# A graph layer and a routed feed-forward in one kernel: the first eight quads of pass one from an early table

## The reference, cut to what matters

```
# layer 1: graph aggregation, then a recurrence over the 128 steps
beta = (layernorm(x) @ e_weight) / max(sum(adj, axis=2), 1e-7)
agg  = einsum('blu,blm->bmu', beta, adj)
h    = tanh(agg[:, t] @ Wx + h @ Wh + b)          # for t = 0 .. 127
x    = x + all the h
# layer 2: 16 experts, the best two per token
y      = layernorm(x)
logits = y @ gate_w + gate_b;  w, idx = softmax/top_k(logits, 2)
moe    = sum over the two of  w * (relu(y @ w1[e] + b1[e]) @ w2[e] + b2[e])
x      = x + layernorm(y + moe) * gamma + beta
```

## Time and profile before

| | |
|---|---|
| median of 3 runs | 655.46 us |
| the profiled execution's own time | 655.11 us |
| its span, first to last instruction | 653.4 us |
| busy: PE, DVE, ACT, POOL | 535.4, 507.6, 411.0, 451.3 us |
| stage B, scatters of POOL | 99 to 264 us |
| pass one, scatters of POOL | 276 to 454 us |
| pass two, scatters of POOL | 471.5 to 648.5 us |

### The profile page before, as it was taken

One profiled execution on the slowest core, in us unless ns is written; L12 is line 12 of the kernel. 1 busy time (PEld: TensorE's weight loads), 2 busy tenths in 40 slices (PEclk: granted clock), 3 DMA queues, 4 the chain that ended last, 5 costly groups with the idle time before them and its releaser, 6 DMA issues. The chain is left out here.

```text
span 653.4 us, 17215 instructions
## 1 busy us (share of the span) xinstructions
PE 535.4 (82%) x4144; PEld 476.4 (73%) x4144; DVE 507.6 (78%) x2512; ACT 411.0 (63%) x1343; POOL 451.3 (69%) x521
## 2 busy tenths in 40 slices
PE   1676799999889861799999999943899999999990
PEld 0566567776666650599999999941799999988890
DVE  4899269999999997488888888620499899898861
ACT  1898765555555533366666666710589889899860
POOL 8766307777777777277777777776177777777775
PEclk9988899889999965899999999975799999999995
DMA  8999913665355214479886665442997666764110
GB/s 208 254 285 271 287 50 102 213 200 170 118 168 114 88 54 124 111 241 346 264 257 198 208 199 188 153 157 72 338 332 246 216 200 204 220 187 140 48 54 15
DMA packets 112893, 119.26 MB, mean 183 GB/s; under 512 B 18346, under 2 KB 97406, under 8 KB 112801
## 3 DMA queue, kind: packets, MB, share of 16 engines
q1 hardware_dynamic: 93056, 73.55, 40.6%
q0 software_dynamic: 17152, 43.03, 18.1%
q10 hardware_dynamic: 2592, 1.64, 0.8%
HBM read 66.51 MB, written 53.77 MB: 184 GB/s over the span
## 5 line engine op out<-in xcount | busy, mean ns | idle before, releaser
L311 POOL DMA_INDIRECT out_dram<-R x136 | 135.0, 993 | 59.4 <-issue 52.2
L311 POOL DMA_INDIRECT rows_by_second<-R x136 | 136.2, 1001 | 54.2 <-issue 33.2
L311 POOL DMA_INDIRECT rows_by_first<-st x128 | 125.9, 984 | 64.4 <-issue 35.6
L1143 PE MATMUL bank<-xT,wr 128*128 128x128 f32 (+1 forms) x1152 | 155.6, 280 | 8.9 <-ACT xT L1218 8.9
L1163 PE MATMUL bank<-W,hs 128*128 x1024 | 156.9, 290 | 0.0
L1143 PEld LDWEIGHTS bank<-xT,wr 128*128 128x128 f32 x1152 | 140.8, 194 | 16.0 <-ACT xT L1218 16.0
L1243 ACT ACTIVATE hs<-bank,wr 128x128 f32<-128x128 f32 x380 | 111.8, 366 | 64.4 <-PE bank L1143 59.3
L1163 PEld LDWEIGHTS bank<-W,hs 128*128 128x128 f32 x1024 | 135.1, 192 | 3.1
L1228 ACT COPY wr<-W1b 128x258 f32 x288 | 103.5, 424 | 0.0
L1328 DVE SCALAR_TENSOR_TENSOR R<-bank,R 128x128 f32<-128x128 f32 x272 | 82.2, 344 | 24.5 <-PE bank L1163 24.5
L670 ACT ACTIVATE HT<-bank,bcol 128x128 f32<-128x128 f32 x128 | 47.0, 367 | 66.6 <-PE bank L573 65.6
(11 more groups left out here) (171 smaller groups left out, 896.2 us busy)
## 6 DMA issues: line engine op xcount, KB each, us to landing
R<-rows_by_second SPq DMA_DIRECT2D x122, 196.0 KB
R<-rows_by_first SPq DMA_DIRECT2D x124, 68.0 KB
xq<-in_x_dram SPq DMA_DIRECT2D x32, 256.0 KB, 4.1
aq<-in_adj_dram SPq DMA_DIRECT2D x32, 256.0 KB, 5.0
x2r<-in_x_dram SPq DMA_DIRECT2D x32, 256.0 KB, 2.9
rows_by_second<-filler SPq DMA_DIRECT2D x2, 1568.0 KB, 7.4
rows_by_second<-filler SPq DMA_DIRECT2D x16, 196.0 KB
rows_by_second<-R POOLq DMA_INDIRECT x136
```

Of the source, the lines that this page charges most:

```text
L311: return nc.gpsimd.indirect_dma_start(dst, bass.IndirectOffsetOnAxis(ap=idx, axis=0), src, None, bounds_check=limit[n], oob_is_err=False)
L1143: i = mm(ps_h[c][h][:, at:at + n], wr[:, u % 2, s, j, c * P:(c + 1) * P], xT[:, u % 2, j * P + lo:j * P + lo + n], start=True, stop=True)
```

## The change

Pass one begins before stage B has ended everywhere. After quad 24 of 32 has been placed (`SEEN = 24`), DVE works out an early table of the blocks that are already full (`early_a`, `early_b`), for 32 blocks (`TAKEN`), which are the first eight quads of pass one (`EARLY = 8`). SP loads them as soon as the scatters of the first 24 quads have landed. The full tables are worked out later, by DVE inside pass one: `table_a` after its quad 3, `table_b` after its quad 5. Quads from 8 on use them. With it:

- The bias splitting (`biases`) moves into stage B, behind step 9. A new small instruction per pair of quads (`shift`) prepares -mean/std.
- In pass one `zed` moves from DVE to ACT, and ACT's relus of pass one move to DVE.
- All 16 filler blocks of the first list are now issued by SP; ACT issued half.
- ACT clears the buffers for mixed quads inside pass one, at its quad 12.
- No idle multiplications ahead of pass one; three instead of one behind the wait ahead of pass two.
- In pass two, the first quad is normalised at once, and not during the second quad.

The core of the diff:

```diff
+    SEEN, EARLY = 24, 8
+    TAKEN = EARLY * QUAD
@@ sp_stages
+            sp.wait_ge(early_tables, 1)
+            for u in range(SLOTS):
+                sp.wait_ge(s_sct[u], 64 * SEEN // SLOTS)
+            for q in range(EARLY):
+                for j, row in enumerate(numbers(sp, sti[0:1, 0, QUAD * q:QUAD * q + QUAD], ROWS - P)):
+                    load(sp, 0, q, j, row)
             sp.wait_ge(starts, 1)
             pad(sp, 0)
+            pad(sp, 8)
@@ dve_stages
+            def shift(p):
+                dve.wait_ge(s_r2, p + 1)
+                v.scalar_tensor_tensor(out=two(p, C_SHIFT), in0=two(p, C_MEAN), scalar=-1.0, in1=two(p, C_RSTD),
+                                       op0=ALU.mult, op1=ALU.mult)
             for t in range(0, NQ + 4, 2):
                 even(t)
                 odd(t + 1)
+                if t == 8:
+                    biases()
+                if t + 1 == SEEN + 3:
+                    early_a()
+                if t + 1 == SEEN + 5:
+                    early_b()
@@ sp_passes
-                rows = [numbers(sp, sti[0:1, r, QUAD * q:QUAD * q + QUAD], ROWS - P) for q in range(AHEAD)]
-                begin(sp, r, rows, (0, 1))
-                for q in range(AHEAD, NQUAD):
+                if r:
+                    rows = [numbers(sp, sti[0:1, r, QUAD * q:QUAD * q + QUAD], ROWS - P) for q in range(AHEAD)]
+                    begin(sp, rows, (0, 1))
+                else:
+                    landed(sp, 0)
+                for q in range(AHEAD if r else EARLY, NQUAD):
                     quad(r, q, q + NQUAD * r, (q + NQUAD * r) % RING)
                     if r == 0 and q == RING - 1:
                         pad_b(sp)
@@ pe_passes
-            pe.wait_ge(tables, 1)
+            pe.wait_ge(early_tables, 1)
+            pe.wait_ge(s_pos, NQ)
...
+                landed(pe, 1)
+                warm(3)
...
+                if G == EARLY:
+                    pe.wait_ge(tables, 1)
...
+                if G == 4:
+                    codes()
@@ act_passes
+            def zed(G, u):
+                act.wait_ge(e_ld[u], loads_of(G))
+                for j in range(QUAD):
+                    i = a(R[:, u, j, C_Z:W_B], R[:, u, j, 0:P], ACT.Identity,
+                          scale=R[:, u, j, C_RSTD:C_RSTD + 1], bias=R[:, u, j, C_SHIFT:C_SHIFT + 1])
+                i.then_inc(e_z, 1)
+            def quad_0(q, G, u, last):
...
+                if q == EARLY - 1:
+                    act.wait_ge(tables, 1)
+                if q == RING:
+                    zeros_for_mixed()
+                e = experts(0, q + 1)
+                v = (u + 1) % RING
+                zed(G + 1, v)
+                weights(0, q + 1, G + 1, v, 0, e)
+                weights(0, q + 1, G + 1, v, 1, e)
+                turn_out(G + 1, v)
+                weights(0, q + 1, G + 1, v, 2, e)
+                weights(0, q + 1, G + 1, v, 3, e)
@@ dve_passes
+            def quad_0(q, G, u, last):
...
+                relu(G, u, 0)
+                if q > 1:
+                    share(0, G - 1, before, 1)
+                relu(G, u, 1)
+                if q > 0:
+                    add_beta(G, u)
+                share(0, G, u, 0)
...
+                if q == 3:
+                    table_a()
+                if q == 5:
+                    table_b()
+            def quad_1(q, G, u, last):
...
+                if q == 0:
+                    norm_b(G, u, 0)
+                    share(1, G, u, 1)
+                    norm_a(G, u, 1)
+                    norm_b(G, u, 1)
```

More of the change, by code:

```diff
@@ L1040, in passes @@
+            return table_a, table_b
         def passes(eng, body):
@@ L1184, in quad @@
                     second(r, G, 0, e[2:4])
+                    second(r, G, 1, experts(r, at + QUAD)[0:2])
                 if not last:
@@ L1257, in experts, with begin_pass @@
                 return e + numbers(act, et_act[0:1, r, at + QUAD:at + 2 * QUAD]) if mixed(q) else e
-            def quad(r, q, G, u, last):
-                start = isinstance(q, int) and q == 0
-                if start:
-                    e = experts(r, q)
-                    for j in range(QUAD):
-                        weights(r, q, G, u, j, e)
-                    loads(r)
-                    turn_out(G, u)
-                if r == 0 and q == NPURE:
+            def begin_pass(r, q, G, u):
+                e = experts(r, q)
+                for j in range(QUAD):
+                    weights(r, q, G, u, j, e)
+                if r:
+                    loads()
+                else:
+                    zed(G, u)
+                turn_out(G, u)
@@ L1268, in quad @@
+            def quad_1(q, G, u, last):
+                start = q == 0
+                if start:
+                    begin_pass(1, q, G, u)
+                if q == NPURE:
                     act.wait_ge(e_mix, 2)
-                e = None if last else experts(r, q + 1)
+                e = None if last else experts(1, q + 1)
                 v = (u + 1) % RING
-                relu(r, G, u, 0)
-                if r == 1 and not start:
+                relu(G, u, 0)
+                if start:
+                    relu(G, u, 1)
+                elif q > 1:
@@ L1273, in quad @@
                     root(G - 1, 0)
+                if not last:
+                    weights(1, q + 1, G + 1, v, 0, e)
+                    weights(1, q + 1, G + 1, v, 1, e)
                 if start:
-                    relu(r, G, u, 1)
-                if not last:
-                    weights(r, q + 1, G + 1, v, 0, e)
-                    weights(r, q + 1, G + 1, v, 1, e)
-                if not start:
-                    relu(r, G, u, 1)
+                    root(G, 0)
+                else:
+                    relu(G, u, 1)
@@ L1281, in quad @@
                 if not last:
                     turn_out(G + 1, v)
-                    weights(r, q + 1, G + 1, v, 2, e)
-                    weights(r, q + 1, G + 1, v, 3, e)
-                if r == 1 and not start:
+                    weights(1, q + 1, G + 1, v, 2, e)
+                    weights(1, q + 1, G + 1, v, 3, e)
+                if q > 1:
                     root(G - 1, 1)
-                if last and r == 1:
+                if start:
+                    root(G, 1)
+                if last:
```

387 lines of the change are left out of this document (227 added, 160 removed).

## The result

The changed kernel takes 667.87 us (median of 4 runs, 666.71 to 668.58) where the kernel before takes 655.61 on the same chip (654.96 to 658.24): ratio 1.0187, 95% interval 1.0163 to 1.0212. It is 1.9% slower. The forecast of 659.5 had the direction; the time lies above the range of 648.5 to 666.

The account below looks back on a forecast made before the run. POOL, issuing scatters, was taken to bound the kernel. On 655.11 us: start +0.3, stage B +6.5, first gap -12.0, pass one +13.1, start of pass two -3.6 gave 659.4, as median 659.5; range 648.5 to 666.

Parts of the forecast that it names:

- (g): Pass one, SP: loads wait for `table_b`, quad 12's also for `pad_b`; POOL stalls 3 us at quad 11.
- (h): Pass one, ACT: clearing buffers for 7.1 us at quad 12 costs 4.8 us, of which 4 are counted.
- (e): Pass one, DVE: `table_a` takes 7.5 us behind quad 3's first half; POOL stalls 3.6 us.
- (f): Pass one, DVE: `table_b` takes 2.9 us with no lead, and PE returns at half clock; together 2.5 us.
- (a): Stage B, DVE: the bias chain of 12 instructions adds 3.0 us.
- (b): Stage B, DVE: `shift`, about 13 times, adds 2.6 us.
- (c): Stage B, DVE: `early_a`, 15 dependent instructions, adds 3.3 us.
- (d): Stage B, DVE: `early_b`, six instructions on 32 numbers, adds 1.3 us.
- Rival 2: Pass one: pauses come but PE does not fall to half clock; 9.5 instead of 13.1 us, 655.8; chance 0.12.
- Rival 3: Pass one: PE's clock stays low, a slow quad follows each pause; 20 us, 666.3; chance 0.10.
- Rival 1: Pass one: added work is covered, PE keeps its clock, `pad_b` takes 10 us; stalls of 3, 649.3; chance 0.23.
- (i): Pass one: exchanging `zed` for relus between DVE and ACT costs neither engine more than 0.3 us per quad.

Follow-up runs that it names:

- e_split_2: e_all with `table_a` cut into four pieces behind quads 0 to 3, run again on another chip: 646.32 us, ratio 0.9862.
- e_all: Changed kernel with `pad_b` issued early, ACT's clearing at quad 26 and the old order at the start of pass two: 650.97 us, ratio 0.9931.
- e_both: Changed kernel with `pad_b` issued early and ACT's clearing moved from quad 12 to quad 26: 652.10 us, ratio 0.9962.
- e_stage: Kernel before with `biases` behind step 9 of stage B and `shift` per pair, its result unused: 657.10 us, ratio 1.0023.
- e_bias_2: e_all with `biases` ahead of the loop of stage B and a semaphore for the `b2k` loads, run again: 648.75 us, ratio 0.9907.
- e_clock: Changed kernel with idle multiplications of PE, 9 ahead of quad 12's transposes and 5 ahead of quad 13's: 663.11 us, ratio 1.0134.
- e_best: e_all with `biases` ahead of stage B and `table_a` in four pieces: 876.60 us, ratio 0.9915, on one chip; 642.32 us, ratio 0.9802, run again.

## Why the prediction was wrong, step by step

The mechanism held in the main: each pause that was named came. Two terms had the wrong size, and they make up the miss: (g) and (h), and the start of pass two.

| step | predicted | measured | from |
|---|---|---|---|
| POOL's preamble | +0.3 | -0.8 | first scatter, within its scatter from run to run |
| stage B (a to d, less the lead) | +6.5 | +6.9 | stage lengths |
| first gap | -12.0 | -12.0 | stage lengths |
| (e), (f) the two tables | +6.1 | +5.2 | e_split_2 against e_all |
| (g), (h) filler list, clearing | +7.0 | +12.8 | e_both against after |
| start of pass two | -3.6 | -0.4 | gap and pass two |

**Stage B** was right as a sum, and (a) with it: 3.0 predicted, 2.9 and 3.3 measured (e_stage; e_bias_2 against e_all). (b) was not: e_stage had `shift` too and shows nothing beyond the biases. (c) and (d) were 4.6 and are 4.2. So of the 3.7 us of lead that I deducted, about 2.6 were what hides `shift`. The traces show it: from the end of `place_3` of quad 23 to POOL's scatter of that quad it is 4.3 us before and 1.7 in e_bias_2, which has `shift` and no biases in the loop, and 0.8 wherever POOL waits for DVE. The biases came at quad 6, where that distance was 2.3 us before, so the lead was still small. The lead can be spent once.

**The tables.** Right in place and nearly in size: `table_a` takes the 7.5 us that were forecast. But (f) had no cost of its own. e_split_2 has `table_b` whole behind quad 5, and POOL has no pause there; the pauses at quads 4 and 5 in the kernel after go with `table_a` as well. The part of the clock is inside the 5.2 us and wasn't measured apart from the wait. PE was granted 0.57 from 286 to 294 us and 1.00 from there to 330.

**(g) and (h), the step that failed.** "Stall 3 us" was a pause of 6.5 with 0.3 of it usual: 6.2. The load itself was forecast to the tenth (about 333, `zed` began at 332.89). What came behind was too short: from the end of `zed` at 334.54 to POOL at 339.30 it is 4.8 us, where I had 337 less 334.2. I had priced PE there at full clock, though PE had idled for 8.28 us. In e_clock, where PE keeps its clock, the same stretch takes 3.3 us (333.83 to 337.11), so 1.5 of the 2.0 us that I had too little are the clock. POOL was also ready 0.6 earlier (333.07), and `zed` on ACT took 1.65 instead of 1.2. In (h) I counted 4 of 4.8 for a lead that the stall in (g) had just consumed. It was 5.9 there and 0.8 more behind it. So the failed step is this: both waits were priced with PE at full clock behind them, which is 3.1 of the 5.8 us by e_clock, and (h) with 0.8 us of lead that was gone; the rest is the longer chain behind `zed` and POOL's being ready sooner.

Rival 2 (stalls without the clock) is out: e_clock shows 3.1 us of clock. Its objection that 1.76 us of idle time is enough was wrong as a rule. After 1.81 us in e_stage the transposes ran at full clock, as they did after 1.75 in e_all (0.66 at 308.50), while after 4.81 and 8.28 us in the kernel after they took 1.12. Rival 3 was right that slow work follows the long waits, but the size is 3.1 at the two long ones, and behind quad 5 the granted clock stayed at 1.00. Its 666.3 us is the nearest to the measured time by luck: it put 20 us into pass one for slow quads behind every pause, where 17.9 were measured for other reasons in the main, and it kept the -3.6 of pass two, of which -0.4 came. Rival 1 (covered) is out for this kernel; e_both shows that it needs both remedies.

**The start of pass two.** The gap was predicted at "near 14 us" and is 14.00, so the -3.6 itself came (-4.4). How much of it the three multiplications gave isn't shown: the 1.7 us that I took for the clock rest on one slow start, and e_stage shows a faster one without them. I didn't ask what stands behind the moved roots in ACT's queue: quad 1's copy and relus, +4.0. The rule I had used in stage B, to name what is queued behind a waiting instruction, was not used here.

(g) and (h) by 5.8, the start of pass two by 3.2 and stage B by 0.4 are 9.4 too little; the tables (0.9) and the first scatter (1.1) were too much. That leaves 7.4, the 7.3 us between +4.3 and +11.6 but for rounding. The median lies another 1.2 above the profiled run, which was the fastest of four.

**(i)** held as far as the sum goes: with the fillers and the table out of the way, pass one is no longer than before (176.16), so the exchange costs nothing there.

## What to carry to other kernels

When work is moved out of a gap into a running pipeline, look for where the engine has a wait or a lead of its own: the biases were free in DVE's 12 us wait and cost 3 in the loop, the clearing was free at quad 26 and cost 6 at quad 12, and the table cost 5 in one piece and nothing in four. A lead pays for one thing only, so list what spends it in order. Read a clock that one profile shows behind one wait in a second profile too, before a price is put on it. And read the in-order queue behind every instruction that is moved forward, on each engine that it touches, before its gain is booked.

## What the hardware showed that I had not expected

- Four `zed` on ACT (`scale` and `bias` from SBUF, 128x128 fp32) take 1.63 to 1.65 us, 484 ns each in the page's mean over 136; four relus on ACT (L1362) take 1.14.
- The kernel before took 654.5 to 655.6 us (medians) on the other chips and 888 on one. The kernel of e_best took 876.60 there and 642.32 elsewhere, with a granted clock in stage B of 0.72 and 0.90, and on that chip with 78.3 us of ACT's waits that the profile doesn't explain. POOL did not set the pace there, so a comparison of such variants has to name the chip's time for the kernel before and the clock under which it was made.
- The same start of pass two, with one multiplication behind the last landing, had its first transposes at 1.12 us after 1.76 us of idle time in the profile of before and at 0.66 after 1.81 in that of e_stage. With three multiplications they took 0.60 to 0.66 in all eleven profiles that have them.
